# One ring of 16 tiles, written in place, with four tiles (4 MB) in each transfer

## The chip, the core and the metric

The kernel runs on one core of a Trainium2 chip. The core has an engine for matrix products (TensorE, in the profile PE, with its weight loads as PEld), one for vectors (VectorE, DVE), one for scalar functions (ScalarE, ACT), a general one (GpSimd, POOL) and one that here only issues transfers (SyncE, SP). The engines run side by side and wait for each other on semaphores. Sixteen DMA engines move data between the chip's memory (HBM) and the core's own memory (SBUF), whose 128 partitions each hold a row of every tile; matrix products land in another memory, PSUM. The metric is the device time of one execution in microseconds. Of the kernel before, three executions gave 324.55, 325.27 and 326.28 us, so a median of 325.27.

## The reference

For each of 128 samples there is an `x` of 128 channels by 1024 times, and a subject, a number from 0 to 7 that picks one of eight 128 by 128 weight matrices. The result is `x` plus the product of `x` with the weights of its subject, over the channels:

```
def reference(x, itok_B_0_7, L0_cond_weights):       # x (128,128,1024) f32, weights (8,128,128) f32
    w = weights[subjects]                             # (128 samples, 128, 128)
    out = einsum('bct,bcd->bdt', x, w)
    return x + out
```

67.1 MB are read and 67.1 MB written, all in float32.

## The kernel before, in words

A tile is two samples, so there are 64 tiles. Two neighbouring channels of a sample lie in one partition (`row` is 2 x 1024 values, 8 KB), so a tile fills 128 partitions: partitions 0 to 63 hold one sample, 64 to 127 the other. A tile is 1 MB.

The eight weight matrices are loaded once (line 76). The unit matrix is added to them (DVE, line 159), so that the product gives `x` plus the mix at once. Then TensorE spreads their rows (line 126) so that the half of a tile's 128 partitions that holds a sample finds the weights of its even and odd channels; DVE and ACT copy the result from PSUM into `table` (lines 164 and 192). Before this, TensorE does eight products that nobody reads (line 120).

Then four engines each run a loop over the 64 tiles, eight tiles to a turn:

- GpSimd reads the subjects of the two samples and copies their weights from `table` into one of four slots of `selected` (line 112).
- TensorE waits for the tile's `x`, for its weights and for a free half of PSUM, and does 8 products, which the trace shows as 16 records because a float32 product goes in two passes (line 144).
- DVE copies the results of the first sample from PSUM to `out_ring` (line 177), ACT those of the second (line 205), two copies each.
- SP issues the loads into `x_ring` and ACT the stores out of `out_ring`. `SPAN` is 2, so each transfer carries two tiles, 2 MB. Both rings have eight tiles.

What orders them: a load (line 85) waits on `product_ready`, that is, until TensorE is done with the two tiles whose place it takes. A store (line 213) waits until both halves of its two tiles have been copied out of PSUM. The copies of the first tile of a pair wait on `stored` (lines 175 and 203) until the store that used this place of `out_ring` one turn ago has landed. So a load never waits for a store. The loads are all in one queue, q1, the stores in another, q10, and both queues are served by the same sixteen DMA engines.

Of the kernel before, what the change touches and what calls it, by code (L numbers as in the profile page):

```python
# [16 lines left out]
HALF = 64  # L17

WARM_MATMULS = 8

# [4 lines left out]
def subject_mix_kernel(nc: bass.Bass, x: bass.AP, subjects: bass.AP, weights: bass.AP, out: bass.AP):  # L25
# [15 lines left out]
    with ExitStack() as ctx:  # L41
        def sem(name):
            return ctx.enter_context(nc.semaphore(name))

        x_ring = ctx.enter_context(nc.sbuf_tensor("x_ring", [channels, TILES_PER_TURN, row], F32))
        out_ring = ctx.enter_context(nc.sbuf_tensor("out_ring", [channels, TILES_PER_TURN, row], F32))
        loaded = ctx.enter_context(nc.sbuf_tensor("loaded", [channels, n_subjects, mixed], F32))
# [3 lines left out]
        spread = ctx.enter_context(nc.sbuf_tensor("spread", [channels, wide], F32))  # L51
        unit = ctx.enter_context(nc.sbuf_tensor("unit", [channels, mixed], F32))
        selected = ctx.enter_context(nc.sbuf_tensor("selected", [channels, SELECT_BUFS, wide], F32))
# [7 lines left out]
        unit_ready = sem("unit_ready")  # L61
        unit_added = sem("unit_added")
        weights_spread = sem("weights_spread")
# [10 lines left out]
        @block.sync  # L74
        def _(sp):
            sp.dma_start(loaded[:], weights.rearrange("n c d -> c n d")).then_inc(weights_loaded, DMA)
            for s in range(0, TILES_PER_TURN, SPAN):
                sp.dma_start(x_ring[:, s:s + SPAN], x_rows[:, s:s + SPAN, :]).then_inc(x_loaded[s // SPAN], DMA)

            with sp.Fori(0, turns - 1) as turn:  # L80
                for s in range(0, TILES_PER_TURN, SPAN):
                    tile = turn * TILES_PER_TURN + s

                    sp.wait_ge(product_ready, PRODUCT_FREE + tile + SPAN)
                    sp.dma_start(x_ring[:, s:s + SPAN], x_rows[:, bass.ds(tile + TILES_PER_TURN, SPAN), :]
                                 ).then_inc(x_loaded[s // SPAN], DMA)

        @block.gpsimd
        def _(pool):
            nc.gpsimd.memset(ones[:], 1.0).then_inc(ones_ready, 1)  # L90
            pool.wait_ge(ones_ready, 1)

            nc.gpsimd.affine_select(unit[:], ones[:, :mixed], [[-1, mixed]],  # L93
                                    ALU.is_equal, 0.0, base=0, channel_multiplier=1).then_inc(unit_ready, 1)

            nc.gpsimd.affine_select(spread[:], ones[:], [[-1, 2], [0, 2], [-2, HALF]],  # L96
                                    ALU.is_equal, 0.0, base=0, channel_multiplier=1).then_inc(spread_ready, 1)
            pool.wait_ge(subjects_loaded, DMA)

            with pool.Fori(0, turns) as turn:  # L100
                for s in range(TILES_PER_TURN):
                    k = s % SELECT_BUFS
                    tile = turn * TILES_PER_TURN + s
                    for g in range(2):
                        part = slice(g * HALF, (g + 1) * HALF)
                        subject = pool.value_load(subject_row[0:1, bass.ds(2 * tile + g, 1)],  # L106
                                                  min_val=0, max_val=n_subjects - 1)
                        pool.wait_ge(table_ready, 2 * banks)
                        if g == 0:

                            pool.wait_ge(product_ready, PRODUCT_FREE + tile - SELECT_BUFS + 1)
                        nc.gpsimd.tensor_copy(selected[part, k:k + 1, :],  # L112
                                              table[part, bass.ds(subject, 1), :]).then_inc(weights_selected, 1)

        @block.tensor
        def _(pe):
            pe.sem_inc(product_ready, PRODUCT_FREE)
            pe.wait_ge(ones_ready, 1)
            for _ in range(WARM_MATMULS):
                nc.tensor.matmul(products[:, 1, 1, :wide], ones[:, :mixed], ones[:], start=True, stop=True)  # L120
            pe.wait_ge(spread_ready, 1)
            for n in range(banks):
                cols = slice(n * BANK, (n + 1) * BANK)
                pe.wait_ge(unit_added, n + 1)
                for e in range(2):
                    nc.tensor.matmul(products[:, 0, e, cols], spread[:, e * channels:(e + 1) * channels],  # L126
                                     loaded[:].rearrange("c n d -> c (n d)")[:, cols], start=True, stop=True
                                     ).then_inc(weights_spread, 1)

            with pe.Fori(0, turns) as turn:  # L130
                for s in range(TILES_PER_TURN):
# [8 lines left out]
                    for n in range(banks):  # L140
                        for e in range(2):
                            for g in range(2):
# [3 lines left out]
                                    selected[part, k, e * mixed:(e + 1) * mixed],  # L146
                                    x_ring[part, s, e * times + n * BANK:e * times + (n + 1) * BANK],
                                    start=(e == 0), stop=(e == 1))
                    last.then_inc(product_ready, 1)

        @block.vector
        def _(dve):
            dve.sem_inc(even_drained, DRAINED_FREE)
            dve.wait_ge(unit_ready, 1)
            dve.wait_ge(weights_loaded, DMA)
            part = n_subjects // banks
            for n in range(banks):
                some = slice(n * part, (n + 1) * part)
                nc.vector.tensor_tensor(loaded[:, some], loaded[:, some],  # L159
                                        unit[:].unsqueeze(1).to_broadcast([channels, part, mixed]),  # L160
                                        ALU.add).then_inc(unit_added, 1)
            for n in range(banks):
                dve.wait_ge(weights_spread, 2 * n + 1)
                nc.vector.tensor_copy(  # L164
                    table[:, n * part:(n + 1) * part, :mixed].rearrange("p n (b m) -> p n m b", b=2),
                    products[:, 0, 0, n * BANK:(n + 1) * BANK].rearrange("p (n m b) -> p n m b", n=part, b=2)
                ).then_inc(table_ready, 1)

            def go_round(turn, first=False):
# [11 lines left out]
            go_round(0, first=True)  # L181
            with dve.Fori(1, turns) as turn:  # L182
                go_round(turn)

        @block.scalar
        def _(act):
            act.dma_start(subject_row[:], subjects.rearrange("(a b) -> a b", a=1)).then_inc(subjects_loaded, DMA)
            act.sem_inc(odd_drained, DRAINED_FREE)
            part = n_subjects // banks
            for n in range(banks):  # L190
                act.wait_ge(weights_spread, 2 * n + 2)
                nc.scalar.copy(  # L192
                    table[:, n * part:(n + 1) * part, mixed:].rearrange("p n (b m) -> p n m b", b=2),
                    products[:, 0, 1, n * BANK:(n + 1) * BANK].rearrange("p (n m b) -> p n m b", n=part, b=2)
                ).then_inc(table_ready, 1)

            def go_round(turn, first=False):
                for s in range(TILES_PER_TURN):
                    tile = turn * TILES_PER_TURN + s
                    act.wait_ge(product_ready, PRODUCT_FREE + tile + 1)  # L200
                    if not first and s % SPAN == 0:

                        act.wait_ge(stored[s // SPAN], turn * DMA)
                    for b in range(2):
                        nc.scalar.copy(out_ring[HALF:channels, s, b * times:(b + 1) * times],  # L205
                                       products[b * HALF:(b + 1) * HALF, s % PSUM_BUFS, 1, :]
                                       ).then_inc(odd_drained, 1)
                    if s % SPAN == SPAN - 1:
# [4 lines left out]
                        act.dma_start(out_rows[:, bass.ds(tile - SPAN + 1, SPAN), :],  # L213
                                      out_ring[:, at:s + 1]).then_inc(stored[s // SPAN], DMA)

            go_round(0, first=True)
            with act.Fori(1, turns) as turn:
                go_round(turn)
            for s in range(0, TILES_PER_TURN, SPAN):
# [17 lines left out]
```

## Time and profile before

| What | Value |
|---|---|
| median of three executions | 325.27 us |
| the profiled execution's own time | 326.1 us |
| its span, first to last instruction | 324.4 us |
| moved | 134.78 MB, 415 GB/s over the span |
| PE, DVE, ACT, POOL busy | 78%, 49%, 41%, 16% |
| mean granted TensorE clock | 0.925 |
| loads, stores of `x` and `out` | 32 and 32, 2048 KB each |

The span is shorter than the time, by 1.7 us, since something happens before the first and after the last instruction. The profile lists for each engine its busy time, for each group of instructions a mean duration and the idle time before it with what ended that, and for the DMA engines the mean busy share and the GB/s in slices of the span. The granted clock is 1.0 where TensorE runs at its upper level (2.4 GHz) and 0.5 at its lower (1.2 GHz).

### The profile page before, as it was taken

Reading aid. Unit: us, or ns where it says so; the run is one execution under the profiler, and the core shown is the slowest. Engines: PE = TensorE matmul, PEld = TensorE weight load, DVE = VectorE, ACT = ScalarE, POOL = GpSimd, SP = SyncE. Lnnn points to the kernel's source line nnn. Section 1 sums busy time; section 2 is a strip of 40 time slices with the busy share of each in tenths; the row PEclk is TensorE's granted clock in tenths of the full one; section 3 lists DMA queues with packets and bytes.
Section 4 is the critical chain, followed back from the end, with each engine's and each line's share of the span. In section 5 each row is a group of like instructions: output and inputs, shape, how many; then the busy total and the mean of one; then the engine's idle time right before and its main releaser. Section 6 shows DMA issues by size and latency. Waiting matters only on the chain.

```text
span 324.4 us, 3929 instructions
## 1 busy us (share of the span) xinstructions
PE 253.9 (78%) x1048; PEld 121.7 (38%) x1048; DVE 159.7 (49%) x132; ACT 132.0 (41%) x131; POOL 51.8 (16%) x136
## 2 busy tenths in 40 slices
PE   8699999979866688686986868876669968688730
PEld 6244444434433334232443433443234434334310
DVE  1256776754356543466352564534662636645250
ACT  1244665653244432344242443432442424434240
POOL 1231221210111111011110111111110101110000
PEclk9899999997999999799897998999996979989785
DMA  7999999999999999999999999999999999999994
GB/s 275 423 417 353 427 427 428 426 427 427 429 426 429 426 428 427 428 427 429 425 429 426 427 426 428 427 428 427 427 428 426 428 427 428 427 429 427 428 425 187
DMA packets 18453, 134.78 MB, mean 415 GB/s; under 512 B 1041, under 2 KB 2066, under 8 KB 2066
## 3 DMA queue, kind: packets, MB, share of 16 engines
q1 hardware_dynamic: 9744, 67.64, 50.1%
q10 hardware_dynamic: 8706, 67.11, 48.9%
q8 instruction: 1, 0.02, 0.0%
q14 instruction: 2, 0.02, 0.0%
HBM read 67.63 MB, written 67.11 MB: 415 GB/s over the span
## 4 chain that ended last, share of the span: by engine, by line
DMA 60%; PE 22%; DVE 7%; issue 5%; DVEq 1%; ACT 1%; POOL 0%; ACTq 0%; POOLq 0%
DMA out<-out_ring 60%; PE products L144 19%; DVE out_ring L177 7%; PE products L120 2%; PE products L126 1%; DVEq L41 1%; ACT table L192 0%; ACT out_ring L205 0%; POOL selected L112 0%; DVEq L182 0%; ACTq L213 0%; POOL ones L90 0%; POOLq L106 0%; DVEq L175 0%; DVEq L172 0%
## 5 line engine op out<-in xcount | busy, mean ns | idle before, releaser
L144 PE MATMUL products<-x_ring,selected 64*128 64x512 f32 x1024 | 244.2, 631 | 55.8 <-DVE out_ring L177 28.2
L177 DVE COPY out_ring<-products 64x1024 f32<-64x1024 f32 x128 | 156.4, 1222 | 145.9 <-PE products L144 75.2
L205 ACT COPY out_ring<-products 64x1024 f32<-64x1024 f32 x128 | 128.6, 1005 | 172.3 <-PE products L144 92.7
L144 PEld LDWEIGHTS products<-x_ring,selected 64*128 64x128 f32 x1024 | 115.4, 200 | 184.6 <-issue 131.5
L112 POOL COPY selected<-table 64x256 f32 x128 | 50.6, 396 | 240.0 <-PE products L144 198.5
L120 PE MATMUL products<-ones 128*128 128x256 f32 x16 | 6.2, 573 | 1.2 <-POOL ones L90 1.2
L120 PEld LDWEIGHTS products<-ones 128*128 128x128 f32 x16 | 4.8, 306 | 2.3 <-POOL ones L90 1.2
L192 ACT COPY table<-products 128x512 f32<-128x512 f32 x2 | 2.1, 1045 | 7.1 <-PE products L126 7.1
L159 DVE TENSOR_TENSOR loaded<-loaded,unit 128x512 f32<-128x512 f32 x2 | 1.3, 688 | 5.0 <-DMA loaded<-weights 5.0
L126 PE MATMUL products<-loaded,spread 128*128 128x512 f32 x8 | 3.6, 593 | 0.0
L164 DVE COPY table<-products 128x512 f32<-128x512 f32 x2 | 2.1, 1048 | 2.8 <-PE products L126 2.8
L126 PEld LDWEIGHTS products<-loaded,spread 128*128 128x128 f32 x8 | 1.5, 190 | 1.5 <-issue 1.4
L192 ACT ACT_TABLE_LOAD x1 | 1.3, 1283 | 1.5 <-PEq L228 1.5
L96 POOL TENSOR_SCALAR_AFFINE_SELECT spread<-ones 128x256 f32<-128x256 f32 x1 | 0.4, 417 | 0.0
L90 POOL MEMSET ones<- 128x256 f32 x1 | 0.3, 312 | 0.3 <-POOLq L228 0.3
L93 POOL TENSOR_SCALAR_AFFINE_SELECT unit<-ones 128x128 f32<-128x128 f32 x1 | 0.3, 292 | 0.1
L228 POOL MEMSET const-float32-0.0<- 128x1 f32 x1 | 0.1, 97 | 0.1
L228 POOL MEMSET const-bfloat16-1.0<- 128x1 bf16 x1 | 0.1, 100 | 0.0
L228 POOL MEMSET const-uint8-127<- 128x1 uint8 x1 | 0.1, 100 | 0.0
L228 POOL MEMSET const-float32-1.0<- 128x1 f32 x1 | 0.1, 98 | 0.0
L228 POOL BASE_LOAD x1 | 0.0, 17 | 0.2 <-issue 0.2
## 6 DMA issues: line engine op xcount, KB each, us to landing
x_ring<-x SPq DMA_DIRECT2D x32, 2048.0 KB, 30.4
out<-out_ring ACTq DMA_DIRECT2D x32, 2048.0 KB, 32.9
loaded<-weights SPq DMA_DIRECT2D x1, 512.0 KB, 4.0
subject_row<-subjects ACTq DMA_DIRECT2D x1, 0.5 KB
```

What stands on the lines that cost most here:

```text
L41: with ExitStack() as ctx:
L96: nc.gpsimd.affine_select(spread[:], ones[:], [[-1, 2], [0, 2], [-2, HALF]], ALU.is_equal, 0.0, base=0, channel_multiplier=1).then_inc(spr ...
L112: nc.gpsimd.tensor_copy(selected[part, k:k + 1, :], table[part, bass.ds(subject, 1), :]).then_inc(weights_selected, 1)
L120: nc.tensor.matmul(products[:, 1, 1, :wide], ones[:, :mixed], ones[:], start=True, stop=True)
L126: nc.tensor.matmul(products[:, 0, e, cols], spread[:, e * channels:(e + 1) * channels], loaded[:].rearrange("c n d -> c (n d)")[:, cols], ...
L144: last = nc.tensor.matmul(products[:, b, g, n * BANK:(n + 1) * BANK], selected[part, k, e * mixed:(e + 1) * mixed], x_ring[part, s, e * ti ...
L159: nc.vector.tensor_tensor(loaded[:, some], loaded[:, some], unit[:].unsqueeze(1).to_broadcast([channels, part, mixed]), ALU.add).then_inc( ...
L164: nc.vector.tensor_copy(table[:, n * part:(n + 1) * part, :mixed].rearrange("p n (b m) -> p n m b", b=2), products[:, 0, 0, n * BANK:(n + ...
L177: nc.vector.tensor_copy(out_ring[0:HALF, s, b * times:(b + 1) * times], products[b * HALF:(b + 1) * HALF, s % PSUM_BUFS, 0, :]).then_inc(e ...
L192: nc.scalar.copy(table[:, n * part:(n + 1) * part, mixed:].rearrange("p n (b m) -> p n m b", b=2), products[:, 0, 1, n * BANK:(n + 1) * BA ...
L205: nc.scalar.copy(out_ring[HALF:channels, s, b * times:(b + 1) * times], products[b * HALF:(b + 1) * HALF, s % PSUM_BUFS, 1, :]).then_inc(o ...
L228: nc = bacc.Bacc("TRN2", target_bir_lowering=False, num_devices=1)
```

## The change

The two rings become one, `ring`, of 16 tiles: as much memory as before. A tile's results are copied from PSUM over its own `x`, and the store reads them there. `SPAN` becomes 4, so there are 16 loads and 16 stores of 4 MB, and four places for them in the ring.

With that, what waits for what changes. The copies out of PSUM wait only for the products. A load waits, on SP, for the landing of the store that empties its place (`stored`). TensorE waits for its `x` once in four tiles.

The preparation is also written anew: the eight products at the start go, the unit matrix is added on the way from PSUM to `table` (two DVE additions over 1024 values a partition in place of two additions and two copies, and two copies on ACT), GpSimd builds the unit matrix already spread, and it waits for the table once, ahead of its loop.

```
-TILES_PER_TURN = 8
-SPAN = 2
+TILES_PER_TURN = 16
+SPAN = 4
-        x_ring = ...sbuf_tensor("x_ring", [channels, TILES_PER_TURN, row], F32)
-        out_ring = ...sbuf_tensor("out_ring", [channels, TILES_PER_TURN, row], F32)
+        ring = ...sbuf_tensor("ring", [channels, TILES_PER_TURN, row], F32)
...
-                    sp.wait_ge(product_ready, PRODUCT_FREE + tile + SPAN)
-                    sp.dma_start(x_ring[:, s:s + SPAN], x_rows[:, bass.ds(tile + TILES_PER_TURN, SPAN), :]
+                    sp.wait_ge(stored[s // SPAN], turn * DMA + DMA)
+                    sp.dma_start(ring[:, s:s + SPAN], x_rows[:, bass.ds(tile + TILES_PER_TURN, SPAN), :]
...
-            for _ in range(WARM_MATMULS):
-                nc.tensor.matmul(products[:, 1, 1, :wide], ones[:, :mixed], ones[:], start=True, stop=True)
             pe.wait_ge(spread_ready, 1)
-            for n in range(banks):
-                pe.wait_ge(unit_added, n + 1)
-                for e in range(2):
+            pe.wait_ge(weights_loaded, DMA)
+            for e in range(2):
+                for n in range(banks):
...
-                nc.vector.tensor_tensor(loaded[:, some], loaded[:, some], unit..., ALU.add)
-                nc.vector.tensor_copy(table[..., :mixed], products[:, 0, 0, n * BANK:(n + 1) * BANK])
+                dve.wait_ge(weights_spread, e + 1)
+                nc.vector.tensor_tensor(table[:, :, e * mixed:(e + 1) * mixed], products[:, 0, e, :], unit..., ALU.add)
...
                     dve.wait_ge(product_ready, PRODUCT_FREE + tile + 1)
-                    if not first and s % SPAN == 0:
-                        dve.wait_ge(stored[s // SPAN], turn * DMA)
-                        nc.vector.tensor_copy(out_ring[0:HALF, s, b * times:(b + 1) * times],
+                        nc.vector.tensor_copy(ring[0:HALF, s, b * times:(b + 1) * times],
...
-                    if not first and s % SPAN == 0:
-                        act.wait_ge(stored[s // SPAN], turn * DMA)
-                        nc.scalar.copy(out_ring[HALF:channels, s, b * times:(b + 1) * times],
+                        nc.scalar.copy(ring[HALF:channels, s, b * times:(b + 1) * times],
```

On SP, in the loop that issues the loads, the program has this in a row before (`product_ready` counts the tiles that TensorE has done):

```order
L80 UNCONDITIONAL_BRANCH
L80 ISA
L85 ISA [waits product_ready]
L85 DMA x_ring<-x 128x2x2048
L85 ISA [waits product_ready]
L85 DMA x_ring<-x 128x2x2048
```

And this of the change (`stored0`, `stored4` are the semaphores of the stores out of the first and the second place of the ring):

```order
L77 UNCONDITIONAL_BRANCH
L77 ISA
L82 ISA [waits stored0]
L82 DMA ring<-x 128x4x2048
L82 ISA [waits stored4]
L82 DMA ring<-x 128x4x2048
```

The load has the same place in the row, but what it waits for has moved from TensorE to the other DMA queue, and it carries twice the tiles.

On ACT, in the loop over the tiles, before:

```order
L205 COPY out_ring<-products 64x1024 [waits stored0]
L205 COPY out_ring<-products 64x1024
L200 REGISTER_ALU
L205 COPY out_ring<-products 64x1024 [waits product_ready]
L205 COPY out_ring<-products 64x1024
L210 ISA
L213 ISA [waits even_drained,odd_drained]
L213 DMA out<-out_ring 128x2x2048
```

And of the change:

```order
L184 COPY ring<-products 64x1024 [waits product_ready]
L184 COPY ring<-products 64x1024
L182 REGISTER_ALU
L184 COPY ring<-products 64x1024 [waits product_ready]
L184 COPY ring<-products 64x1024
L182 REGISTER_ALU
L184 COPY ring<-products 64x1024 [waits product_ready]
L184 COPY ring<-products 64x1024
L189 ISA
L192 ISA [waits even_drained,odd_drained]
L192 DMA out<-ring 128x4x2048
```

The wait for an earlier store is gone from the copies, and a store is issued behind the copies of four tiles, not of two.

## Rows read from the trace of the kernel before

**Rows 1.** The page: span in 40 slices, busy tenths and GB/s
```profile
DMA  7999999999999999999999999999999999999994
GB/s 275 423 417 353 427 427 428 426 427 427 429 426 429 426 428 427 428 427 429 425 429 426 427 426 428 427 428 427 427 428 426 428 427 428 427 429 427 428 425 187
```

**Rows 2.** Windows: busy us of each engine, granted clock, DMA share, GB/s
```profile
1.80:2.00 0.20, 0.20 (x2) 0.18 (x1) 0.00 (x0) 0.20 (x1) 0.12 (x1) 1.00 0.03 10
...
4.00:24.00 20.00, 17.21 (x61) 9.08 (x61) 7.53 (x8) 5.81 (x6) 4.74 (x12) 0.91 1.02 424
24.80:26.70 1.90, 1.90 (x11) 0.85 (x10) 1.00 (x1) 1.00 (x1) 0.39 (x1) 1.00 1.02 423
26.70:29.70 3.00, 3.00 (x16) 1.43 (x14) 2.01 (x3) 1.58 (x3) 0.79 (x2) 1.00 1.04 276
60.00:300.00 240.00, 189.04 (x784) 89.11 (x782) 120.36 (x99) 99.18 (x99) 37.99 (x96) 0.94 1.01 428
302.00:319.00 17.00, 8.83 (x32) 4.17 (x32) 4.89 (x4) 4.02 (x4) 0.00 (x0) 0.74 1.01 426
```

**Rows 3.** Windows: the end of the span
```profile
320.00:321.00 1.00, 0.00 (x0) 0.00 (x0) 0.00 (x0) 0.00 (x0) 0.00 (x0) 0.50 0.10 41
...
323.20:323.40 0.20, 0.00 (x0) 0.00 (x0) 0.00 (x0) 0.00 (x0) 0.00 (x0) 0.50 0.00 0
```

**Rows 4.** Waits: engine, line, waited for: us in total, times, longest
```profile
ACT out_ring L205 <- DMA out<-out_ring: 77.7, 17, 5.7
PE products L144 <- DMA x_ring<-x: 13.3, 6, 2.8
```

**Rows 5.** The chain that ended last, in order of time: start, us, what
```profile
257.02 0.03 issue
...
262.32 34.43 DMA out<-out_ring
...
296.85 0.10 DVE out_ring L177
```

**Rows 6.** Line 213, the stores: from issue to landing
```profile
DMA to landing us min/median/max: 10.3/32.9/34.5
```

**Rows 7.** Timeline: issues of transfers and ACT's copies, at start and end
```profile
0.87 0.45 SPq L76 DMA_DIRECT2D loaded<-weights  x1
24.84 0.43 ACTq L213 DMA_DIRECT2D out<-out_ring  x1
...
307.48 2.04 ACT L205 COPY out_ring<-products 64x1024 f32<-64x1024 f32 x2 [6.13 <-PE products L144]
310.91 2.04 ACT L205 COPY out_ring<-products 64x1024 f32<-64x1024 f32 x2 [1.40 <-PE products L144]
313.61 0.38 ACTq L213 DMA_DIRECT2D out<-out_ring  x1
```

**Rows 8.** Timeline of PE: two pairs of tiles near the end
```profile
272.30 7.14 PE L144 MATMUL products<-x_ring,selected 64*128 64x512 f32 x32 [1.12 <-ACT out_ring L205]
...
302.04 8.83 PE L144 MATMUL products<-x_ring,selected 64*128 64x512 f32 x32 [2.77 <-DVE out_ring L177]
```

**Rows 9.** Line 78, the first four loads: from issue to landing
```profile
DMA to landing us min/median/max: 8.5/15.0/22.2
```

**Rows 10.** Timeline: preparation and the first tile
```profile
1.23 6.23 PE L120 MATMUL products<-ones 128*128 128x256 f32 x16 [1.23 <-POOL ones L90]
4.96 1.29 DVE L159 TENSOR_TENSOR loaded<-loaded,unit 128x512 f32<-128x512 f32 x2 [4.96 <-DMA loaded<-weights]
7.29 3.60 PE L126 MATMUL products<-loaded,spread 128*128 128x512 f32 x8
10.92 1.04 ACT L192 COPY table<-products 128x512 f32<-128x512 f32 x1 [0.67 <-PE products L126]
18.84 2.47 DVE L177 COPY out_ring<-products 64x1024 f32<-64x1024 f32 x2 [7.72 <-PE products L144]
```

More of the change, by code:

```diff
@@ L17 @@
 HALF = 64
-WARM_MATMULS = 8
 DRAINED_FREE = 2 * PSUM_BUFS
@@ L43, in sem @@
             return ctx.enter_context(nc.semaphore(name))
-        x_ring = ctx.enter_context(nc.sbuf_tensor("x_ring", [channels, TILES_PER_TURN, row], F32))
-        out_ring = ctx.enter_context(nc.sbuf_tensor("out_ring", [channels, TILES_PER_TURN, row], F32))
+        ring = ctx.enter_context(nc.sbuf_tensor("ring", [channels, TILES_PER_TURN, row], F32))
         loaded = ctx.enter_context(nc.sbuf_tensor("loaded", [channels, n_subjects, mixed], F32))
@@ L77, in _ @@
             for s in range(0, TILES_PER_TURN, SPAN):
-                sp.dma_start(x_ring[:, s:s + SPAN], x_rows[:, s:s + SPAN, :]).then_inc(x_loaded[s // SPAN], DMA)
+                sp.dma_start(ring[:, s:s + SPAN], x_rows[:, s:s + SPAN, :]).then_inc(x_loaded[s // SPAN], DMA)
             with sp.Fori(0, turns - 1) as turn:
@@ L91, in _ @@
             pool.wait_ge(ones_ready, 1)
-            nc.gpsimd.affine_select(unit[:], ones[:, :mixed], [[-1, mixed]],
-                                    ALU.is_equal, 0.0, base=0, channel_multiplier=1).then_inc(unit_ready, 1)
             nc.gpsimd.affine_select(spread[:], ones[:], [[-1, 2], [0, 2], [-2, HALF]],
                                     ALU.is_equal, 0.0, base=0, channel_multiplier=1).then_inc(spread_ready, 1)
+            pool.wait_ge(spread_ready, 1)
+            for g in range(2):
+                part = slice(g * HALF, (g + 1) * HALF)
+                if g:
+                    pool.wait_ge(unit_ready, g)
+                nc.gpsimd.affine_select(unit[part, :], ones[part, :], [[1, 2], [-1, mixed]],
+                                        ALU.is_equal, 0.0, base=0, channel_multiplier=2).then_inc(unit_ready, 1)
             pool.wait_ge(subjects_loaded, DMA)
+            pool.wait_ge(table_ready, 2)
             with pool.Fori(0, turns) as turn:
@@ L117, in _ @@
             pe.sem_inc(product_ready, PRODUCT_FREE)
-            pe.wait_ge(ones_ready, 1)
-            for _ in range(WARM_MATMULS):
-                nc.tensor.matmul(products[:, 1, 1, :wide], ones[:, :mixed], ones[:], start=True, stop=True)
             pe.wait_ge(spread_ready, 1)
-            for n in range(banks):
-                cols = slice(n * BANK, (n + 1) * BANK)
-                pe.wait_ge(unit_added, n + 1)
-                for e in range(2):
-                    nc.tensor.matmul(products[:, 0, e, cols], spread[:, e * channels:(e + 1) * channels],
-                                     loaded[:].rearrange("c n d -> c (n d)")[:, cols], start=True, stop=True
-                                     ).then_inc(weights_spread, 1)
+            pe.wait_ge(weights_loaded, DMA)
+            for e in range(2):
+                for n in range(banks):
+                    cols = slice(n * BANK, (n + 1) * BANK)
+                    last = nc.tensor.matmul(products[:, 0, e, cols], spread[:, e * channels:(e + 1) * channels],
+                                            loaded[:].rearrange("c n d -> c (n d)")[:, cols], start=True, stop=True)
+                last.then_inc(weights_spread, 1)
             with pe.Fori(0, turns) as turn:
@@ L146, in _ @@
                                     selected[part, k, e * mixed:(e + 1) * mixed],
-                                    x_ring[part, s, e * times + n * BANK:e * times + (n + 1) * BANK],
+                                    ring[part, s, e * times + n * BANK:e * times + (n + 1) * BANK],
                                     start=(e == 0), stop=(e == 1))
@@ L153, in _ @@
             dve.sem_inc(even_drained, DRAINED_FREE)
[L154 to L169, printed above, removed]
+            dve.wait_ge(unit_ready, 2)
+            for e in range(2):
+                dve.wait_ge(weights_spread, e + 1)
+                nc.vector.tensor_tensor(
+                    table[:, :, e * mixed:(e + 1) * mixed].rearrange("p n (b m) -> p n m b", b=2),
+                    products[:, 0, e, :].rearrange("p (n m b) -> p n m b", n=n_subjects, b=2),
+                    unit[:, e * mixed:(e + 1) * mixed].rearrange("p (m b) -> p m b", b=2).unsqueeze(1).to_broadcast(
+                        [channels, n_subjects, HALF, 2]),
+                    ALU.add).then_inc(table_ready, 1)
+            with dve.Fori(0, turns) as turn:
                 for s in range(TILES_PER_TURN):
@@ L188, in _ @@
             act.sem_inc(odd_drained, DRAINED_FREE)
[L189 to L197, printed above, removed]
+            with act.Fori(0, turns) as turn:
                 for s in range(TILES_PER_TURN):
@@ L213, in go_round @@
                         act.dma_start(out_rows[:, bass.ds(tile - SPAN + 1, SPAN), :],
[L214 to L218, printed above, removed]
+                                      ring[:, at:s + 1]).then_inc(stored[s // SPAN], DMA)
             for s in range(0, TILES_PER_TURN, SPAN):
```

7 lines of the change are left out of this document (1 added, 6 removed).

## The prediction

> **What bounds the kernel now.** I read the slices first: the DMA engines are 90% busy or more in every slice but the first and the last, at 425 to 429 GB/s from 32 us on [rows 1]. PE, at 78%, is busiest of the rest, and the waits show that it seldom lacks `x` (13.3 us in all), while ACT waits 77.7 us for earlier stores to land, and DVE much the same [rows 4]. So the transfers are the bound, and the stores' queue is the late one: a store takes 34.43 us from issue to landing [rows 5], though a 2 MB store issued late took 10.3 [rows 6].
>
> Next the windows, for holes. Loads alone moved 424 GB/s (4 to 24 us), both kinds 428, stores alone 426 [rows 2]. There is one weak stretch, 276 GB/s for 3 us, starting 1.9 us after the first store's issue at 24.84 [rows 2, 7]: (428 - 276)/428 x 3.0 = 1.1 us lost, once. At the end there is no hole: the last store is issued at 313.61 [rows 7], and the DMA engines move 426 GB/s right through 302 to 319 [rows 2], since older stores are still queued. From 320 us only some 41 GB/s are left, one or two engines of sixteen (428/16 = 27 each) finishing late, and past 323.2 nothing [rows 3]. The last landing is at 313.61 + 10.3 = 323.9, 0.5 us ahead of the end of the span. So before is one unbroken transfer. It can be made shorter only by a higher rate, and longer by any hole. That is the question to ask of the change: does the queue run dry anywhere?
>
> **The change, part by part.** *Bytes and packets.* Bytes are the same, and the contiguous pieces too (8 KB, `row`). Only the number of transfers falls, 64 to 32. With both queues filled the rate shows no gap between transfers, so I cost this at 0.
>
> The Trainium skill, "DMA: Bandwidth & Descriptors", section Bandwidth, speaks for a gain: it gives 341 GB/s for a 1 MB transfer and 425 for 16 MB, and asks for large ones. The trace shows 428 with 2 MB, because the queues overlap the fixed cost; a gain of that kind is the second rival.
>
> *Preparation.* The weights land at 4.9 (DVE starts at 4.96), the spreading products took 3.60 us at the upper clock, and the eight products ahead of them ran slowly (6.23 us for half as wide ones) [rows 10]. Without these, the spreading starts near 5.0 at the lower clock, at most 2 x 3.6 = 7.2 us: done by 9 to 12.2. An addition of 1024 values from PSUM is about two copies of 512, 2 x 1.04 = 2.1, so the table is ready by 11 to 14.3. Before, the table was done at 10.92 + 1.04 = 12.0 and the first tile at 18.84, which less 5.4 for a slow tile (below) puts its start 1.4 later. The first tile can start at 13 to 16. It also needs its load: the slowest of the first four 2 MB loads took 22.2 us, a median one 15.0, a quick one 8.5 [rows 9], and 4 MB at 424 GB/s are 9.9 us, so with 0.5 MB of weights ahead from 2.0 us on, and the landing, the first lands near 14. Start: about 15 instead of 13.4. All of it lies beside loads that keep the DMA engines full, so it costs 0.
>
> *First stores, first reloads.* Tiles come every 3.43 us (310.91 - 307.48), the first in 5.4, and from the last product to the issue is 313.61 - 310.91 = 2.70 [rows 7]. Store 1: 15 + 5.4 + 3 x 3.43 + 2.7 = 33.4, in motion 1.9 later, 35.3. The four opening loads alone would end at 14 + 3 x 9.9 = 43.7; the 8.4 us left share the engines with store 1, so they end at about 52. Store 1 (4.19 MB at half of 428, 19.6 us, less what it gains once the loads are through) ends at about 53.5; the weak stretch puts 1.1 on both. Store 2 is issued at 33.4 + 4 x 3.43 = 47.1, in time. So the engines don't run dry here. But load 5 can be issued only when store 1 has landed, when the loads' queue is empty.
>
> *The turnaround x.* From a store's last byte to the first byte of the load it frees: last byte to landing, 323.3 to 323.9 = 0.6 [rows 3, 6], the waiter's wake 0.1 (262.32 + 34.43 = 296.75, and DVE goes at 296.85 [rows 5]), and issue to first byte, 1.1 (0.87 to 2.0) or, under traffic, 1.9 (24.84 to 26.7) [rows 2, 7]; between two ends so near I take the middle, 1.5. x = 2.2, bounds 1.8 and 2.6. During x store 2 has the engines alone and gains x/2 over its half share, and load 5 starts x late: it ends 2x after store 2. From there both queues stay filled and share equally, so load k+3 keeps ending 2x after store k, up to load 16 after store 13.
>
> *The end.* When load 16's last byte is in, stores 14 and 15 are left, less what store 14 got in 2x at half share. Two 4 MB stores take half a turn of before, (296.75 - 257.02)/2 = 19.87 us [rows 5] (the same store one turn apart, late in the span, so at the slow engine's pace). Left: 19.87 - x = 17.7 us of work. Meanwhile the last four tiles go from load to store: 0.6 to landing, 0.1 wake, the compute, 1.5 to the first byte. PE has then waited 19.9 - 4 x 3.43 = 6.1 us less what a slow start takes, some 4. After a wait of 2.8 a pair took 8.83 us, after 1.1 it took 7.14 [rows 8], and the first tile of the slow pair took 307.48 - 302.04 = 5.44 [rows 7, 8]; the mean granted clock from 302 to 319 is 0.74 [rows 2]. So compute = 5.44 + 3 x 3.43 + 2.70 = 18.4, and the way is 0.6 + 0.1 + 18.4 + 1.5 = 20.6. The hole is 20.6 - 17.7 = 2.9 us. Before had none since its last pair needed 11.57 us (302.04 to 313.61) with several older stores still queued.
>
> The cost hidden until now is the serial tail of a group of four; its cover is the two older stores, and it is 3 us too short. The removed waits (ACT and DVE on stores) give nothing, since what they waited for is the same DMA work; SP waits for it now, with nothing behind it but loads that have to wait as well.
>
> *Sum.* Span 324.4 + 2.9 = 327.3, and with the 1.7 outside it 329.0 for the profiled execution, 0.9% over its 326.1. That execution is 0.8 over the median of 325.27; on the median: 328.2.
>
> *Bounds.* Low: the upper clock throughout (7.14 for the first pair, so compute 7.14 + 2 x 3.43 + 2.70 = 16.7), first byte after 1.1, and the load lag only x (if loads end after store 1): the way 18.5, left 19.87 - 0.9 = 19.0, no hole, 325.3. High: two slow tiles (compute 20.4), x 2.6, first byte 1.9: 23.0 - 17.3 = 5.7, 331.0.
>
> On the clock the Trainium skill, "TensorE: Matmul & The Clock Gate", section "Part 1: The HAM clock gate", says that an idle engine falls to half clock and a busy one comes back; the rows agree only in part, since waits of 1.1 and 2.8 us had different outcomes. By the rule, the wait of some 4 us makes the slow start certain, and the sum stays.
>
> **Rivals.**
> 1. *The cover is long enough: no change.* PE at the upper clock makes the way 18.9 us and the hole 1.2; a lag of x rather than 2x (opening loads that end after store 1) takes another 1.1. Time 325.3 to 326.5. For it: some pairs did run in 7.14, and whether the loads' queue is empty when store 1 lands is a matter of 1 or 2 us in my sum. Against: PE waits longer than before ahead of each group.
> 2. *Faster: larger transfers raise the rate.* Place: between 30 and 300 us. If all went at the best slice, 429 instead of 427.5 [rows 1], 134.78 MB take 1.1 us less, and the weak stretch's 1.1 may go as well; with no hole 323.1. It decides only if the hole is under half a microsecond. Against: nothing in the rows shows a gap between transfers.
> 3. *The turnaround is far longer than x.* The weak stretch ended 4.9 us after the store's issue; if the first bytes come only then, x = 5.6, the way is 24.0, left are 14.3: hole 9.7, 335.0. For it: those 3 us. Against: the rate drops at 1.9, so something of the store is in motion by then.
>
> **How the numbers follow.** The measurement tells about 0.5%, 1.6 us, from no change. The forecast has 0.63 (326.9 to 331.0), the first rival 0.23, the second 0.05, the third 0.09. Slower by over 0.5% is forecast and third rival, 0.72; same the first, 0.23; faster the second, 0.05. The range, 325.2 to 331.5, leaves out most of the second and third.
>
> **What would show it.** In the profile after: DMA slices at 9 up to about 310 us, then one weak slice just before the last store, with about 3 us in which the engines move next to nothing between store 15's end and store 16's first byte; PE waiting for `ring` some 4 us before every group; SP's waits all on stores; store 16 issued 18.4 us after PE starts on the last group; DVE and ACT waiting for PE alone. I would be wrong if stores 14 and 15 still moved when store 16 was issued and for 1.5 us more, if the rate between 60 and 300 us were not 428, or if a slice in the first 60 us were empty.

## The result, and the profile after

Four executions of the changed kernel took 330.09 to 331.92 us, median 330.65, against 325.33 for the kernel before on the same chip: the ratio is 1.0158 (95% interval 1.0126 to 1.0191), 5.3 us slower. 328.2 was forecast, in a range of 325.2 to 331.5. The direction and the place were right, the size was not: the hole ahead of the last store is about twice as long as forecast.

The page of the changed kernel: span, slices of the span, and the chain that ended last.

```profile
span 328.5 us, 3698 instructions
...
DMA  7999999999999999999999999999999999999538
GB/s 273 426 417 428 416 429 428 429 422 428 429 429 428 431 422 429 429 429 428 431 423 428 430 428 429 431 421 430 429 429 428 431 421 430 430 428 429 249 144 367
...
DMA 60%; PE 32%; issue 2%; DVE 1%; DVEq 1%; SPq 0%; ACTq 0%
```

Beside [rows 1], the third last and the second last slice (304 to 320 us) are at 249 and 144, where before has 428 and 425. The fourth slice rose from 353 to 428, where before had its weak stretch. The rest is alike. In windows (busy us by engine, granted clock, DMA share, GB/s):

```profile
24.00:30.00 6.00, 6.00 (x32) 2.88 (x30) 4.89 (x4) 4.02 (x4) 1.58 (x4) 1.00 1.01 421
60.00:300.00 240.00, 189.62 (x768) 89.16 (x766) 118.17 (x97) 100.78 (x100) 38.39 (x97) 0.88 1.01 428
300.00:308.00 8.00, 8.00 (x35) 4.09 (x34) 3.42 (x3) 2.98 (x3) 0.00 (x0) 0.89 1.01 427
308.00:311.40 3.40, 3.40 (x18) 1.78 (x16) 2.41 (x3) 1.98 (x3) 0.00 (x0) 1.00 0.21 89
311.40:317.20 5.80, 2.46 (x12) 0.89 (x8) 3.95 (x4) 3.08 (x4) 0.00 (x0) 1.00 0.00 0
317.20:327.20 10.00, 0.00 (x0) 0.00 (x0) 0.00 (x0) 0.00 (x0) 0.00 (x0) 0.58 0.99 412
```

From 60 to 300 us the rate is 428, as before [rows 2]. Most DMA engines run dry near 308.4, the slowest at 311.4, and nothing moves for 5.8 us after that. (Full rate is back at 317.5.) What the core does in this time is the serial tail of the last group. The timeline of PE for the last two groups, ACT's issues of the last two stores, and the chain's piece for load 16 (start, us, what):

```profile
278.40 15.43 PE L143 MATMUL products<-ring,selected 64*128 64x512 f32 x64 [3.03 <-DMA ring<-x]
298.15 15.70 PE L143 MATMUL products<-ring,selected 64*128 64x512 f32 x64 [4.33 <-DMA ring<-x]
```
```profile
296.56 0.38 ACTq L192 DMA_DIRECT2D out<-ring  x1
316.58 0.38 ACTq L192 DMA_DIRECT2D out<-ring  x1
```
```profile
267.21 30.58 DMA ring<-x
297.79 0.37 issue
298.15 15.71 PE products L143 x64
```

Load 16 lands at 297.79, PE starts at 298.15, and the last store is issued at 316.58: 18.43 us from PE's start, and 18.4 was forecast. So the way (from the last byte of load 16 to the first byte of the last store) was right, and the cover (the work of the older stores that is left meanwhile) was wrong.

The waits have changed places as the change says (for [rows 4]):

```profile
ACT ring L184 <- PE products L143: 174.6, 64, 17.7
PE products L143 <- DMA ring<-x: 55.4, 13, 9.3
```
```profile
SPq L82 <- DMA out<-ring: 249.0, 12, 44.6
```

### The profile page after: what moved, and what is told of

It is laid out like the page before. It is cut to its first block, busy times and chain, and to the rows that moved or that the text cites. A ratio compares the mean times of both kernels' runs of the same rounds, so it can differ in the third digit from the quotient of the medians.

```text
span 328.5 us, 3698 instructions
## 1 busy us (share of the span) xinstructions
PE 253.3 (77%) x1032; PEld 119.5 (36%) x1032; DVE 160.1 (49%) x130; ACT 133.8 (41%) x132; POOL 52.4 (16%) x137
## 4 chain that ended last, share of the span: by engine, by line
DMA 60%; PE 32%; issue 2%; DVE 1%; DVEq 1%; SPq 0%; ACTq 0%
PE products L143 32%; DMA ring<-x 31%; DMA out<-ring 29%; DVE ring L169 1%; DVEq L39 1%; SPq L73 0%; DVEq L163 0%; SPq L82 0%; ACTq L192 0%; ACTq L190 0%
## 5 line engine op out<-in xcount | busy, mean ns | idle before, releaser
L143 PE MATMUL products<-ring,selected 64*128 64x512 f32 x1024 | 248.1, 645 | 55.4 <-DMA ring<-x 55.4
L169 DVE COPY ring<-products 64x1024 f32<-64x1024 f32 x128 | 156.4, 1222 | 147.5 <-PE products L143 145.5
L184 ACT COPY ring<-products 64x1024 f32<-64x1024 f32 x128 | 128.6, 1005 | 176.2 <-PE products L143 174.6
L143 PEld LDWEIGHTS products<-ring,selected 64*128 64x128 f32 x1024 | 117.5, 206 | 186.0 <-issue 170.7
L125 PE MATMUL products<-loaded,spread 128*128 128x512 f32 x8 | 5.2, 808 | 5.2 <-DMA loaded<-weights 5.2
L156 DVE TENSOR_TENSOR table<-products,unit 128x1024 f32<-128x1024 f32 x2 | 3.7, 1940 | 8.8 <-PE products L125 8.8
L98 POOL TENSOR_SCALAR_AFFINE_SELECT unit<-ones 64x256 f32<-64x256 f32 x2 | 0.8, 402 | 0.1
```

Source lines behind the costliest of these rows:

```text
L98: nc.gpsimd.affine_select(unit[part, :], ones[part, :], [[1, 2], [-1, mixed]], ALU.is_equal, 0.0, base=0, channel_multiplier=2).then_inc(u ...
L125: last = nc.tensor.matmul(products[:, 0, e, cols], spread[:, e * channels:(e + 1) * channels], loaded[:].rearrange("c n d -> c (n d)")[:, ...
L143: last = nc.tensor.matmul(products[:, b, g, n * BANK:(n + 1) * BANK], selected[part, k, e * mixed:(e + 1) * mixed], ring[part, s, e * time ...
L156: nc.vector.tensor_tensor(table[:, :, e * mixed:(e + 1) * mixed].rearrange("p n (b m) -> p n m b", b=2), products[:, 0, e, :].rearrange("p ...
L169: nc.vector.tensor_copy(ring[0:HALF, s, b * times:(b + 1) * times], products[b * HALF:(b + 1) * HALF, s % PSUM_BUFS, 0, :]).then_inc(even_ ...
L184: nc.scalar.copy(ring[HALF:channels, s, b * times:(b + 1) * times], products[b * HALF:(b + 1) * HALF, s % PSUM_BUFS, 1, :]).then_inc(odd_d ...
```

## The experiments

Each ratio below is to the kernel before on the same chip, with its 95% interval. The kernel before ran beside them each time: its median was 326.75 us beside the stores of two tiles, the ring with transfers of 2 MB, the two rings and the preparation, 325.09 beside the single splits and the pieces, and 325.43 beside the ring alone, the fixed reloads and both splits, with single executions from 324.45 to 328.60. So compare ratios, not medians. Names: store k and load k are the k-th of the 16 transfers of 4 MB; a lag is the time from one's landing to the other's; a hole is a stretch in which the DMA engines move less than the 428 GB/s because nothing is queued for them.

**The last store split.** The direct test of the place: only the very last store is cut in two.

```
-            with act.Fori(0, turns) as turn:   # every store: four tiles
+            with act.Fori(0, turns - 1) as turn:
+                go_round(turn)
+            go_round(turns - 1, split=3)       # group 3 of the last turn: two stores of two tiles
```

> The changed kernel with the very last store issued as two of two tiles; all others carry four. Theory A (the loss is the idle stretch ahead of the last 4 MB): its first half is issued near 309.7 and takes 4.9 us of the hole; 325.7 to 326.5, and the lag stays near 10. Rival B: 330.7, since the last tile's store can't land earlier than its issue at 316.6 and the DMA engines are needed in full before.

Measured: 325.51 us, ratio 1.0007 (0.9986 to 1.0028). Windows at its end:

```profile
308.00:312.00 4.00, 4.00 (x22) 1.91 (x20) 3.01 (x3) 2.55 (x4) 0.00 (x0) 1.00 0.49 205
312.00:316.00 4.00, 2.26 (x12) 0.76 (x8) 2.98 (x4) 2.58 (x3) 0.00 (x0) 1.00 0.96 395
316.00:317.60 1.60, 0.00 (x0) 0.00 (x0) 0.77 (x1) 0.33 (x1) 0.00 (x0) 0.70 0.03 10
317.60:319.00 1.40, 0.00 (x0) 0.00 (x0) 0.00 (x0) 0.00 (x0) 0.00 (x0) 0.50 0.91 380
```

The stretch that was empty (312 to 316) now moves 395 GB/s, the first half of the store; a hole of 1.6 us stays. One transfer cut in two takes back the whole loss within the interval (the time is just under the range expected), so the loss was in the hole.

**The first store split.** The same cut at the other end, which tests where the loads' lag comes from.

```
-            with act.Fori(0, turns) as turn:
+            go_round(0, split=0)               # group 0 of the first turn: two stores of two tiles
+            with act.Fori(1, turns) as turn:
+                go_round(turn)
...
-                    sp.wait_ge(stored[s // SPAN], turn * DMA + DMA)
+                    sp.wait_ge(stored[s // SPAN], turn * DMA + (DMA if s else 2 * DMA))
```

> The changed kernel with the very first store issued as two of two tiles; all others carry four. Theory A (the lag of the loads is set once, because the loads' queue was empty when store 1 landed): store 1 starts 6.9 us earlier and lands near 53.7 us, before load 4 ends, so the lag of load 5 behind store 2 falls from 9.9 to about 5 and stays; load 16 leaves 2.5 us more of stores, the hole shrinks by that, 328.0 to 328.5. Rival B (the lag is not set by the opening, but by sharing in each turn): the lag is back near 10 within the span and the time at 330.7.

Measured: 328.41 us, ratio 1.0125 (1.0092 to 1.0157). The interval overlaps that of the changed kernel, so the times alone show it only weakly; the traces show it plainly. SP issued load 5 at 52.7 us, while load 4 was still in motion: between 52.7 and 58 us the loads' queue (q1) moved as many packets as the stores' (q10), with no break. By the landings in the trace, load 5 came 6.2 us after store 2 (about 5 was expected) and load 16 5.6 after store 13; in the changed kernel these were 9.9 and 11.1. Stores 14 and 15 landed at 301.9 and 311.9, in the changed kernel at 302.1 and 312.1, but load 16 landed at 294.8 instead of 297.8, and the last store was issued at 313.60 instead of 316.58. So a lag made in the first 60 us is carried to the end, as the prediction had it. The queues' packets, MB and share from 52.7 to 58 us:

```profile
q10 hardware_dynamic: 143, 1.17, 52.1%
q1 hardware_dynamic: 146, 1.08, 48.7%
```

**All stores of two tiles, loads of four.**

```
+STORE = 2
...
-                    if s % SPAN == SPAN - 1:
+                    if s % STORE == STORE - 1:
```

> The changed kernel, but each store carries two tiles; loads stay at four, and a load waits for both stores of its place. Theory A (the loss is the hole ahead of the last store): the last four tiles' first half is issued near 309.7 us, before the older stores are through, and fills the hole up to some 316; only about 1 to 2 us of it stay, and the time falls from 330.65 to 325.5 to 327. Rival B (the loss is spread: in-place writing or 4 MB loads slow the whole span): the time stays within 1 us of 330.65.

Measured: 325.25 us, ratio 0.9966 (0.9934 to 0.9998). It has both splits' effects: the last store is issued at 315.02, before the one ahead of it lands at 318.35, and load 5 comes 5.2 us after store 2 is through. Loads of 4 MB cost nothing that the interval shows.

**The ring in place with transfers of 2 MB.**

```
-SPAN = 4
+SPAN = 2
```

> The changed kernel with SPAN 2: one ring of 16 tiles in place, but transfers of 2 MB, so eight places. Theory A: the way of the last pair is about 13.5 us and over 20 us of older stores are queued, so no hole; 325.3, give or take 1, and the late part of the ring's places keeps the loads' queue filled from the start. Rival B (in-place writing, with loads that wait for stores, costs by itself): 328 or more.

Measured: 325.02 us, ratio 0.9958 (0.9929 to 0.9987). The DMA slices are at 9 until the last. SP's first reload is issued at 42.89, when opening loads are still in motion. Together with the last three experiments it puts the loss on the size of the stores at the two ends, not on the ring.

**The ring in place alone**, on the kernel before: old preparation, `SPAN` 2.

```
-        x_ring = ...; out_ring = ...            # 8 tiles each
+        ring = ...                              # 16 tiles
-                    sp.wait_ge(product_ready, PRODUCT_FREE + tile + SPAN)
+                    sp.wait_ge(stored[s // SPAN], turn * DMA + DMA)
```

> The kernel before with the one ring of 16 tiles in place, and nothing else: SPAN stays 2 and the preparation is the old one. Theory A (in-place use costs nothing by itself; its 16 opening tiles even keep the loads' queue filled past the first store, so the weak stretch of before at 24 to 30 us goes): no hole, no weak stretch, 324.5 to 325.2, and a scatter of under 1 us. Rival B (the gain of 0.4% seen with SPAN 2 in place came from the new preparation): 325.5 to 326.8, like before.

Measured: 325.48 us, ratio 0.9979 (0.9955 to 1.0004), of twelve executions 324.59 to 325.98. The scatter of 1.4 us and the median miss the figures expected. The ring neither costs nor, beyond doubt, gains. Of the weak stretch little is left: 407 GB/s from 24 to 30 us, where the kernel before has 325. And with the new preparation the same ring and `SPAN` gave 0.9958 (the experiment above), so beside sixteen opening tiles the preparation costs nothing that is seen.

**Two rings with transfers of 4 MB.**

```
-SPAN = 2
+SPAN = 4
```

> The kernel before with SPAN 4 and nothing else: two rings of eight tiles, so only two places of 4 MB in each. Theory A: a place is held by 15.7 us of products, 4 to 5 us of turnaround and 19.6 us of transfer at half share, 39.8 us and more for two places against 39.3 us of transfers, and the store side needs about 42: holes in every turn, 335 to 350 us. Rival C (the size of the transfers is harmless as such, only the in-place ring with its wait on stores makes the hole): 327 to 330.

Measured: 345.65 us, ratio 1.0588 (1.0528 to 1.0647). Windows:

```profile
24.00:32.00 8.00, 8.00 (x40) 3.82 (x38) 5.21 (x5) 4.34 (x5) 1.78 (x5) 1.00 0.02 7
60.00:300.00 240.00, 191.41 (x760) 88.52 (x758) 116.79 (x96) 96.10 (x96) 37.20 (x94) 0.86 1.01 420
324.00:332.00 8.00, 4.56 (x22) 2.00 (x18) 5.09 (x5) 4.03 (x4) 0.00 (x0) 1.00 0.02 7
```

With two places of 4 MB the opening loads end at 24 us, the first place is free at 32, and the 8 us between are empty. In the long middle only 428 - 420 = 8 GB/s are lost, 8/428 x 240 = 4.5 us, so the arithmetic of holes "in every turn" was too dark; the opening and the end, with 8 us each, make most of it. So 4 MB cost far less in one ring with four places than in two with two each.

**The preparation alone**, on the kernel before.

```
-            for _ in range(WARM_MATMULS): ...   # and additions to loaded, four copies to table
+            # spreading products at once, two additions from PSUM to table, unit matrix spread by GpSimd
```

> The kernel before with the new preparation alone (no eight products at the start, unit matrix added on the way to the table, one wait for the table). All theories: the first tile starts near 15.4 us instead of 13.7, and loads fill the DMA engines over this; 325.3, within 0.5. If the preparation had a share in the loss, 326.5 or more.

Measured: 328.51 us, ratio 1.0070 (1.0040 to 1.0101). A miss: I had expected no cost. Windows of this kernel, then of the kernel before:

```profile
24.00:30.00 6.00, 6.00 (x32) 2.86 (x30) 4.88 (x4) 4.02 (x4) 1.59 (x4) 1.00 0.80 258
30.00:34.00 4.00, 4.00 (x22) 1.94 (x20) 2.44 (x3) 2.01 (x2) 0.79 (x2) 1.00 0.97 371
```
```profile
24.00:30.00 6.00, 6.00 (x30) 2.85 (x28) 4.05 (x4) 3.18 (x4) 1.18 (x3) 1.00 1.00 325
30.00:34.00 4.00, 4.00 (x20) 1.83 (x18) 2.98 (x4) 2.55 (x4) 0.80 (x3) 1.00 1.01 420
```

With an `x_ring` of eight tiles the opening loads have landed by 25.3 us. The first reload waits for the first two tiles; it was issued at 22.41 before and at 24.25 here, and the DMA engines lack work (share 0.80): (325 - 258)/428 x 6 = 0.9 us more than before in the first window, and (420 - 371)/428 x 4 = 0.5 in the second. That is the whole difference of the two profiled spans, 325.8 - 324.4 = 1.4 us; the ratio of 0.7% is somewhat more. In the changed kernel the same preparation is hidden by sixteen opening tiles, and costs nothing (421 GB/s in the first window).

**Reloads with fixed addresses**, on the kernel before: an attempt to find what makes its weak stretch.

```
+            reload(0)                           # four loads with fixed addresses
+            with sp.Fori(1, turns - 1) as turn:
+                reload(turn)
```

> The kernel before with the first four reloads (tiles 8 to 15) written out with fixed addresses, so that only the later ones take theirs from a register. Theory D (the weak stretch of before at 24 to 30 us comes from reloads with addresses from registers): it goes, 324.3 or so. Rival E (it comes from the opening ring of eight tiles, whose loads end near 24 us when the first reload, issued at 22.4, is only just arriving): it stays, and the time is that of before.

Measured: 325.43 us, ratio 1.0005 (0.9983 to 1.0027). Its profile has no weak stretch (421 GB/s from 24 to 30 us), yet by its median it is no faster than the kernel before, so neither theory fits. But the edit isn't all that differs between the two profiles. The eight products at the start, which it leaves alone, took 5.12 us here and 6.23 before, and the reloads were issued earlier; here, then before:

```profile
19.73 7.23 SPq L85 DMA_DIRECT2D x_ring<-x  x2
```
```profile
22.41 7.24 SPq L85 DMA_DIRECT2D x_ring<-x  x2
```

So this is no clean test of the addresses. Set side by side, the later the first reload comes, the more is lost from 24 to 34 us, with opening loads that have landed at 25.3 to 25.5 us in all three: nearly nothing when it comes at 19.73 (this kernel), about 1.5 us at 22.41 (before), 2.9 at 24.25 (the preparation alone). That speaks for rival E's place. It isn't shown that the lack of a load is the mechanism: in the kernel before the DMA share stays at 1.00 in this window, so its engines were busy and moved less. Only one execution of each kernel has a profile; whether the stretch comes and goes between executions is open.

**Pieces of 4 KB, in the stores, and in the loads.** What makes a new transfer late behind the other queue? Two kernels cut the rows in halves, one in the stores, one in the loads.

```
-                        act.dma_start(out_rows[:, tiles, :], ring[:, at:s + 1])
+                        for half in (slice(0, times), slice(times, row)):
+                            act.dma_start(out_rows[:, tiles, half], ring[:, at:s + 1, half])
```

> The changed kernel with each 4 MB store issued as two stores of 2 MB that take the left and the right half of every row, so that the contiguous pieces of the stores are 4 KB; the loads keep pieces of 8 KB. In the changed kernel load 5 had its first bytes 3.8 us after its issue, though only a store was in motion. Theory A (a new transfer waits behind some 13 pieces that each DMA engine has already taken from the other queue): with pieces half as long this falls to about 2 us, the lag of load 5 behind store 2 from 9.9 to some 6, the hole by some 2, and the time by 2 to 328 or 329, if the rate holds. Rival B (the 3.8 us are a fixed time of issuing): 3.8 us and 330 to 331, or more if the rate falls. The first store, behind loads of 8 KB, keeps its 3.6 us by both.

> The mirror image: the loads are two of 2 MB with 4 KB pieces each, the stores keep 8 KB. Theory A: load 5, behind store pieces of 8 KB, keeps its 3.8 us, while the first store, behind loads of 4 KB pieces, has its first bytes 2 us after its issue instead of 3.6; the time stays near 330.7. Rival B (fixed time): both stay as they were. Rival C (the time goes into making the new transfer's own descriptors, of which there are twice as many for loads): load 5 takes 5 us or more, and the first store 3.6.

First the delay. The queues' packets, MB and share, in windows from the issue on. The changed kernel, 56.1 to 59.7 and 59.7 to 62 us, around load 5 (issued at 56.17):

```profile
q10 hardware_dynamic: 187, 1.53, 100.7%
...
q10 hardware_dynamic: 61, 0.50, 52.3%
q1 hardware_dynamic: 60, 0.49, 50.5%
```

With stores in pieces of 4 KB, 56.1 to 60.0 and 60 to 62 us, around its load 5 (issued at 56.09):

```profile
q10 hardware_dynamic: 412, 1.63, 101.7%
...
q1 hardware_dynamic: 63, 0.52, 60.9%
q10 hardware_dynamic: 86, 0.35, 43.4%
```

And with loads in pieces of 4 KB, 33.9 to 37.4 us, behind its first store (issued at 33.86):

```profile
q1 hardware_dynamic: 359, 1.40, 100.4%
```

A load waits 3.8 us behind stores of 8 KB pieces and 4.1 behind 4 KB pieces, while 187 and 412 packets, and a few more, go by; the first store waits some 3.6 us behind loads of either kind. (Load 5 of the second kernel is no test: it was issued at 53.45, when opening loads were still in motion, so its queue wasn't empty.) So the delay doesn't go with the number of packets ahead: theory A fell. It isn't a fixed time of issuing alone either, since the last store of the changed kernel, issued to idle DMA engines at 316.58, moved within a microsecond (317.2 to 327.2 has 412 GB/s). It is a delay of a transfer that starts an empty queue while the other is in motion. What is behind it I haven't settled; a backlog counted in bytes would fit as well (1.6 to 1.7 MB went by ahead of load 5 in both kernels).

Then the times, which miss all that was expected: 327.33 us, ratio 1.0034 (0.9995 to 1.0073) for the stores, and 340.40, ratio 1.0439 (1.0366 to 1.0511) for the loads. With both queues filled, the one with 8 KB pieces now moved 0.52 MB against 0.35 (60 to 62 us above). In the second kernel, from 37.5 to 39 us, it is the stores' queue that has the 8 KB pieces and moves more:

```profile
q10 hardware_dynamic: 53, 0.43, 68.9%
q1 hardware_dynamic: 55, 0.23, 36.8%
```

So the length of the pieces sets the share. Loads that get more come early, and the lag is gone (load 5 landed 1.2 us after store 2); loads that get less leave nothing to store at the end. The windows of that second kernel:

```profile
292.00:300.00 8.00, 8.00 (x40) 4.09 (x39) 5.11 (x5) 4.24 (x5) 1.67 (x5) 1.00 1.02 428
300.00:324.00 24.00, 19.40 (x80) 8.83 (x76) 12.13 (x11) 9.97 (x11) 1.49 (x4) 0.86 0.54 225
324.00:328.00 4.00, 0.00 (x0) 0.00 (x0) 2.30 (x2) 1.86 (x2) 0.00 (x0) 1.00 0.16 66
```

**Both ends split.**

```
+            go_round(0, split=0)
+            with act.Fori(1, turns - 1) as turn:
+                go_round(turn)
+            go_round(turns - 1, split=3)
```

> The changed kernel with both its first and its last store issued as two of two tiles. Theory A (the hole was way less cover; either split mends part of it): the lag is near 6 as with the first split alone, the last but one store ends near 312, the first half of the last fills to 317, and the hole is that of the last split alone, about 1 us or less: 325.0 to 325.6, so no sum of the two gains (2.2 and 5.1), since the hole can't become negative. Rival B (each split takes off its own cost): 323.3.

Measured: 324.71 us, ratio 0.9974 (0.9953 to 0.9996). The window from 312 to 316 us has 293 GB/s, (428 - 293)/428 x 4 = 1.3 us of hole. The time lies between the theories, under the range of A and over the figure of B. By the profiled spans the first split gains 3.0 us (328.5 to 325.5), the last 4.7 (323.8) and both 6.4 (322.1), so most of the two adds up. By the ratios (1.0158, and 1.0125, 1.0007 and 0.9974 with the splits) all of it does, but their intervals are too wide to tell. This kernel, the in-place ring with transfers of 2 MB (0.9958) and the one with stores of two tiles (0.9966) are the three whose intervals lie under 1, by 0.3 to 0.4%; among themselves their intervals overlap. For the latter two this is less scatter and not a better best case: they took 324.76 to 325.89 us, and the kernel before beside them 324.45 to 328.60.

## Why the prediction was right, and what was wrong in it

**What bounds the kernel.** Right. The rate between 60 and 300 us is 428 before and after; the change could only add a hole or fill one.

**The way of the last group.** Right. From load 16's landing to the issue of the last store it took 316.58 - 297.79 = 18.8 us against 0.1 + 18.4; with 0.7 at most ahead of the landing, and 0.9 to the first bytes (316.58 to 317.5) instead of 1.5, 20.4 in all against 20.6. PE's slow start came as assumed: the last group took 15.70 us, where 4 x 3.43 = 13.7 would be the quick one; no group that PE had to wait for took less than 15.4.

**The turnaround x.** This step failed. "Issue to first byte, 1.1 or, under traffic, 1.9; between two ends so near I take the middle, 1.5." Load 5's first bytes came 3.8 us after its issue, and x was 4.5, not 2.2, outside my bounds of 1.8 and 2.6. The 1.9 was read off the total rate, which fell 1.9 us after the first store's issue at 24.84; but the rate says nothing about whose bytes move. (Nor was this stretch a lack of work: its DMA share is 1.04 [rows 2], so the engines were busy and moved less.) Split by queue, the trace of the kernel before has this for 24.8 to 28.9 and 28.9 to 30 us:

```profile
q1 hardware_dynamic: 178, 1.45, 106.4%
...
q1 hardware_dynamic: 20, 0.16, 58.3%
q10 hardware_dynamic: 14, 0.11, 24.7%
```

No store packet before 28.9; the first comes at 29.1, after 4.3 us. My third rival took 4.9 from the same stretch, and was nearer for load 5. It was wrong for the last store, which finds the engines idle and starts at once, so its 335 was too much.

**The lag and the cover.** The form was right, and the size followed x. The opening was as forecast but for 1 or 2 us: store 1 issued at 33.63 (33.4), load 4 landed at 53.6 (about 52) and store 1 at 56.0 (53.5, and 1.1 more), so the loads' queue was empty as assumed. The rule "load 5 ends 2x after store 2, and the lag stays" gives 9.0 with x = 4.5; 9.9 was measured, and 9.8 to 9.9 for the next five loads. It crept to 11.1 by load 16, which the rule didn't have. Load 16's last byte was in at about 297.8 - 0.7 = 297.1, so the cover left was 311.4 - 297.1 = 14.3 us of stores against 17.7 forecast: 3.4 less.

**The hole.** 20.4 - 14.3 = 6.1 us on the slowest DMA engine, 311.4 to 317.5, against 2.9. This is more than the 5.7 of the high bound. That the time of 330.65 lies in the range all the same is in part luck: the kernel before had a loss of its own, which went, and which the sum had kept.

**What I left out of the sum.** The weak stretch of the kernel before, (428 - 325)/428 x 6 = 1.4 us from 24 to 30, didn't come back; the same window after lost 0.1. That the 1.1 "may go as well" stood only with the second rival. Hole less stretch is 6.1 - 1.3 = 4.8; the spans differ by 4.1, the medians by 5.3. The spans can be settled by counting all that is lost at the end, which the kernel before has too, since there some engines finish late. Before, then after:

```profile
300.00:324.40 24.40, 8.83 (x32) 4.17 (x32) 6.68 (x6) 5.34 (x6) 0.00 (x0) 0.71 0.82 348
```
```profile
300.00:328.50 28.50, 13.86 (x61) 6.77 (x58) 9.77 (x8) 8.04 (x8) 0.00 (x0) 0.80 0.66 278
```

(428 - 348)/428 x 24.4 = 4.6 us before and (428 - 278)/428 x 28.5 = 10.0 after, 5.4 more; less the 1.3 this is 4.1, the difference of the spans. On the medians 0.8 is added, since the profiled execution of the kernel before was that much above its median. The 0.3 us more outside the span (330.51 - 328.5 = 2.0, before 1.7) I can't explain.

**Bytes, packets, preparation.** No gain from larger transfers, as said. The reason, two queues that cover for each other, is not the only one: one queue alone moved 424 and 426 GB/s with several 2 MB transfers in it [rows 2]. The preparation cost nothing in this kernel, but the reason given was too general: on the kernel before, with its eight opening tiles, it cost 0.7%.

**Rivals.** No change: refuted by the measurement; one of its conditions, opening loads that end after store 1, is what the split of the first store made, and it was worth half of the hole, not all. Faster: no gain in rate was seen.

## What to carry to other kernels

When DMA engines are the bound, compare two times at the end: from the last load's last byte to the last store's first (landing, compute of one group, its copies out of PSUM, issue), and the work of the stores still queued. A larger transfer lengthens the first by whole tiles; here it was enough to split the last transfer alone. And count the reload's turnaround at the moment when its queue is empty: here the lag made there wasn't made good later.

Read first bytes off the packets of the one queue, never off the total rate.

## What the runs showed of the hardware that I had not expected

- A transfer that starts an empty queue while the other queue is in motion moved its first bytes 3.5 to 4.3 us after issue, with 2 MB (27.04 to 30.57 us in the kernel with the first store split; 24.84 to 29.11 before) or 4 MB (56.17 to 59.9 in the changed kernel) and with pieces of 4 or 8 KB; with idle DMA engines it took about 0.9 (316.58 to 317.5).
- With both queues filled, 8 KB pieces against 4 KB pieces moved 0.52 MB against 0.35 in 2 us, and 0.43 against 0.23 in 1.5 us; with equal pieces 0.50 and 0.49.
- The sixteen DMA engines don't finish together, and a landing waits for the last: in the changed kernel the rate falls from 426 GB/s to 188 from 308 to 309 us, 74 in the next and 25 in the one after, about one engine's share, and ends at 311.4; before, 41 GB/s were left from 320 to 321 us and the end came at 323.2 [rows 3]. The rows don't name the engine, so it isn't shown that it is always the same.
